# Attention with 16 heads: stacking transfers in three portions around those of the maxima, q and k split sooner, gate rows stored in the first step

## The reference

```python
h = _layernorm(x, axis=-1) * (1 + ca) + sa
q = (x @ Wq + bq).reshape(B, S, H, Dh)
latent = x @ Wl + bl
k = (latent @ Wk + bk).reshape(B, S, H, Dh)
v = (latent @ Wv + bv).reshape(B, S, H, Dh)
scores = jnp.einsum('bihd,bjhd->bhij', q, k) * SCALE
attn = jax.nn.softmax(scores, axis=-1)
out = jnp.einsum('bhij,bjhd->bihd', attn, v).reshape(B, S, D)
out = out @ Wo + bo
x = x + ga * out
```

## Time and profile before

| what | value |
|---|---|
| median of 3 runs | 931.98 us (923.66, 931.98, 932.79) |
| profiled execution | 924.53 us, of which the span of the core 922.8 us |
| PE busy, mean granted clock | 765.3 us (83%), 0.894 |
| DVE / ACT / POOL busy | 633.5 / 538.8 / 390.3 us |
| first attention, steps 2 to 17 | 45.75 to 351 us of the span |

### The profile page before, as it was taken

How to read it: one execution, slowest core, us unless ns; L and a number is a source line. 1 busy time by engine, 2 the same in 40 slices (tenths; PEclk the granted TensorE clock), 3 DMA queues, 4 the chain that set the end, 5 groups by cost and what they waited for, 6 DMA issues and landing times. The chain is left out here.

```text
span 922.8 us, 17153 instructions
## 1 busy us (share of the span) xinstructions
PE 765.3 (83%) x5738; PEld 516.2 (56%) x5738; DVE 633.5 (69%) x1423; ACT 538.8 (58%) x1195; POOL 390.3 (42%) x484
## 2 busy tenths in 40 slices
PE   3378879899778788678999999848999875999996
PEld 3223323233233322277998999836777654887884
DVE  3086775768686664368677776437888875888885
ACT  0215654556465555367788888537888653555553
POOL 3533442443353300014222100058999762776674
PEclk9998886779797886679999999979999996999998
DMA  4255544333443330030000000000000070355430
GB/s 134 36 86 70 69 64 53 47 48 63 57 68 51 49 36 2 15 116 1 2 1 2 1 1 2 1 2 1 2 2 2 1 187 3 104 145 151 115 103 23
DMA packets 81178, 44.19 MB, mean 48 GB/s; under 512 B 7121, under 2 KB 79298, under 8 KB 80962
## 3 DMA queue, kind: packets, MB, share of 16 engines
q1 hardware_dynamic: 81090, 43.07, 24.3%
HBM read 27.83 MB, written 2.25 MB: 33 GB/s over the span
## 5 line engine op out<-in xcount | busy, mean ns | idle before, releaser
L597 DVE TENSOR_REDUCE att_negmax<-att_p_max 128x2 f32<-128x512 f32 x256 | 172.4, 690 | 97.4 <-PE att_p_max L481 93.3
L681 ACT ACTIVATE att_probs<-att_p_sT 128x1024 f32<-128x1024 f32 x128 | 130.9, 1025 | 111.8 <-PE att_p_sT L487 109.4
L481 PE MATMUL att_p_max<-att0p_QK 48*128 48x256 bf16 x512 | 115.6, 325 | 58.6 <-DMA att0p_QK<-att_parts 43.8
L2053 POOL TENSOR_TENSOR moe_z_lo<-moe_z,moe_z_hi 128x512 fp32r<-128x512 f32 x64 | 96.4, 1517 | 56.3 <-ACT moe_z_hi L2006 55.5
L481 PEld LDWEIGHTS att_p_max<-att0p_QK 48*128 48x128 bf16 x512 | 31.0, 100 | 150.3 <-DVE att_negmax L597 61.1
L487 PE MATMUL att_p_sT<-att0p_QK 51*128 51x256 bf16 x512 | 114.5, 324 | 0.0
L509 PE MATMUL att_p_o<-att_probs,att0p_V 128*32 128x256 f32 x1024 | 102.1, 479 | 0.3 <-ACT att_probs L681 0.3
L944 POOL TENSOR_TENSOR ffn0s_rstd<-ffn0s_var_eps,top_minus_half 128x2 f32<-128x2 f32 x16 | 11.2, 700 | 195.3 <-DVE ffn0s_var_eps L931 195.3
L898 PE MATMUL ffn0s_p_h<-ffn0s_u_hi,top_ffn_all 128*128 128x256 f32 x256 | 69.5, 305 | 16.6 <-DVE ffn0s_u_lo L1159 16.2
L1159 DVE TENSOR_TENSOR ffn0s_g_lo<-ffn0s_g,ffn0s_g_hi 128x512 fp32r<-128x512 f32 x64 | 49.1, 782 | 42.5 <-ACT ffn0s_g_hi L1103 41.1
L2044 DVE TENSOR_TENSOR moe_z<-moe_act_u,top_ffn_all 128x512 f32<-128x512 f32 x64 | 74.2, 1160 | 2.2
(11 more groups left out here) (250 smaller groups left out, 2004.8 us busy)
## 6 DMA issues: line engine op xcount, KB each, us to landing
top_ffn_all<-combine SPq DMA_DIRECT2D x32, 512.0 KB, 6.5
att0p_QK<-att_parts SPq DMA_DIRECT2D x192, 64.0 KB
top_X<-in_L_attn_x SPq DMA_DIRECT2D x4, 512.0 KB, 7.1
att_raw<-in_L_ffn_h_w SPq DMA_DIRECT2D x8, 256.0 KB, 4.7
out_x<-top_X SPq DMA_DIRECT2D x8, 256.0 KB, 2.3
top_wo_all<-gates SPq DMA_DIRECT2D x4, 256.0 KB
top_gbo_all<-gates SPq DMA_DIRECT2D x4, 256.0 KB
top_wo_all<-gates SPq DMA_DIRECT2D x1, 1024.0 KB, 6.1
```

The lines of the kernel that those rows point to most:

```text
L481: mm = pe.matmul(bank(at)[:, i, :], QK[r][rows, g, 0, i * P:(i + 1) * P], QK[r][rows, g, 1, :], start=True, stop=True)
L597: dve.tensor_reduce(negmax[:, :, w, g], bank(at)[:], AX.X, ALU.max, negate=True).then_inc(drained, 1)
L681: act.activation(probs[g % 2][:, t % 2], p_sT[t % 2][:], ACT.Exp).then_inc(exped, 1)
L2053: pool.tensor_tensor(z_lo[e % RING][:], z[e % RING][:], z_hi[e % RING][:].bitcast(F32), ALU.subtract).then_inc(z_lo_ready, 1)
```

## The change

`sp_stack` is called in three portions. In step n SP first sends the portions of batch n-1 that need piece 0 and piece 1 (2 and 6 transfers), then the maxima of batch n-3, then the portion that needs piece 2 (4 transfers). The wait for the buffer and for all earlier stacking transfers stands ahead of portion 0. The maxima's two transfers get a semaphore each, the half that PE reads first goes first, and PE waits for each half by itself. ACT makes piece 0 at slot 10, right behind q and k, instead of slot 13. DVE takes the statistics after slot 6 instead of 8. SP stores the gate rows in step 0 instead of step 1.

```diff
-DVE = {"negmax": 0, "out": 5, "stats": 8, "O": 14}
-ACTS = {"OTn": 1, "maxT": 1, "hT": 6, "qk": 10, "OT": 10, "v": 12, "parts": 13}
+DVE = {"negmax": 0, "out": 5, "stats": 6, "O": 14}
+ACTS = {"OTn": 1, "maxT": 1, "hT": 6, "qk": 10, "parts": 10, "OT": 10, "v": 12}
...
-        max_stacked = sem("max_stacked")
+        max_stacked = [sem(f"max_stacked{w}") for w in range(2)]
...
                 if t == 0:
-                    pe.wait_ge(max_stacked, 32 * (sb_ + 1))
+                    pe.wait_ge(max_stacked[sw], 16 * (sb_ + 1))
...
-            at_least(act, max_stacked, 32 * b)
+            for w in range(2):
+                at_least(act, max_stacked[w], 16 * b)
...
+                if slot == ACTS["parts"] and batch_valid(f):
+                    act_parts(act, f, r)
                 if slot == ACTS["OT"] and batch_valid(t):
                     act_OT(act, t)
                 if slot == ACTS["v"] and batch_valid(f):
                     act_v(act, f, r)
-                if slot == ACTS["parts"] and batch_valid(f):
-                    act_parts(act, f, r)
...
-            for w in range(2):
+            for w in (1, 0):
...
-                             ).then_inc(max_stacked, 16)
+                             ).then_inc(max_stacked[w], 16)
...
-        def sp_stack(sp, b, r):
-            at_least(sp, scoredT, PAIRS * (b - NB + 1))
-            at_least(sp, stacked, 16 * STACK_DMAS * b)
-            for part, ready in enumerate((part0_ready, part1_ready, part2_ready)):
-                sp.wait_ge(ready, b + 1)
...
+        def sp_stack(sp, b, r, part):
+            if part == 0:
+                at_least(sp, scoredT, PAIRS * (b - NB + 1))
+                at_least(sp, stacked, 16 * STACK_DMAS * b)
+            sp.wait_ge((part0_ready, part1_ready, part2_ready)[part], b + 1)
...
         def sp_step(sp, n):
+            if n == 0:
+                sp.wait_ge(gate_rows_ready, 1)
+                sp.dma_start(k.gates_dram, gate_rows[:]).then_inc(gates_stored, 16)
+            if batch_valid(n - 1):
+                sp_stack(sp, n - 1, (n - 1) % NB, 0)
+                sp_stack(sp, n - 1, (n - 1) % NB, 1)
             if batch_valid(n - 3):
                 sp_max(sp, n - 3, (n - 3) % NB)
             if batch_valid(n - 1):
-                sp_stack(sp, n - 1, (n - 1) % NB)
+                sp_stack(sp, n - 1, (n - 1) % NB, 2)
             if n == 1:
-                sp.wait_ge(gate_rows_ready, 1)
-                sp.dma_start(k.gates_dram, gate_rows[:]).then_inc(gates_stored, 16)
                 sp.wait_ge(gates_stored, 16)
```

More of the change, by code:

```diff
@@ L733, in term_source @@
                            [[width, HALF], [(3 + k_part - q_part) * S, 2], [1, S]])
-        def sp_stack(sp, b, r):
-            at_least(sp, scoredT, PAIRS * (b - NB + 1))
-            at_least(sp, stacked, 16 * STACK_DMAS * b)
-            for part, ready in enumerate((part0_ready, part1_ready, part2_ready)):
-                sp.wait_ge(ready, b + 1)
[L740 to L746, removed]
-        def sp_step(sp, n):
+        def sp_stack(sp, b, r, part):
[3 more added lines that the diff above has]
+            sp.wait_ge((part0_ready, part1_ready, part2_ready)[part], b + 1)
+            for n, of in enumerate(TERMS):
+                if max(of) != part:
+                    continue
+                for w in range(2):
+                    rows = slice(w * HALF + n * DH0, w * HALF + (n + 1) * DH0)
+                    sp.dma_start(QK[r][rows], term_source(r, w, n)).then_inc(stacked, 16)
+        def sp_step(sp, n):
+            if n == 0:
[4 more added lines that the diff above has]
+                sp_stack(sp, n - 1, (n - 1) % NB, 1)
             if batch_valid(n - 3):
```

## The result

The changed kernel's median is 898.02 us (893.75 to 906.78, four runs) against 932.38 us of the kernel before on the same chip: ratio 0.9655, 95% interval 0.9604 to 0.9705. Some executions of a kernel are 1.5% or more above its fastest; the medians here include them, the ratios leave them out, and where a profiled execution is such a one (sp_order_old and before_poolwait) only the kind of its waits is read from it. The profiled execution of the changed kernel took 898.87 us with a span of 897.1 us, 25.7 us less than the one before.

The account below looks back on a forecast made before the run. A loop through SP (maxima, then twelve stacking transfers) was taken to set the 19.6 us step. 12 x (19.6 - 18.6) plus 1 plus 2 minus 0.5 gave 14.5, say 15 us: 928.2 - 15 = 913 us, range 882 to 933.

Parts of the forecast that it names:

- the stacking wait: PE, first attention: waits for stacking transfers go from every step behind the third, from 43.8 to under 15 us.
- DVE's chain: Step start, four DVE operations meeting POOL's: 2.0 to 2.2 us instead of 1.4, PE waiting 1.8 us at slot 2.
- the clock: PE behind the slot 2 wait: three steps in four lose full clock, at 3.1 us each, adding 2.3 us per step.
- The eight transfers: SP's queue, pieces 0 and 1 ahead of the maxima: cost put at nothing, up to 1 us per step if cover fails.
- my rival "slower": Slot 8: maxima wait behind piece 1's six transfers, slack 0.7 to 2.8 us; 14 us slower, 942 us; chance 7%.
- the step at full clock: Steps 4 to 15: about 16.3 us each if the clock is never lost, with a wait of 1.8 us in it.
- The first steps: Opening steps: 1 us gained together (bounds -2 and +3), with one wait of 1 to 2 us at slot 8.
- Step 16: Late step of about 20 us with a stacking wait of some 2.6 us behind it: 2 us gained.
- the step after it: Step behind step 16: starts with an uncontended chain, no gain, 0.5 us lost.
- the rival that the clock holds: Steps 4 to 15: chain 1.4 us or less, steps 15.7 to 16.3 us, gain 46 us, 882 us; chance 25%.
- The rival that the wait only moves: Steps 4 to 15: every step behaves as step 8, 20.0 us; time 926 to 930 us; chance 13%.

Follow-up runs that it names:

- sp_order_old: Changed kernel with SP's old order, the maxima first and then all twelve stacking transfers: 927.05 us, ratio 0.9943 to the kernel before.
- before_poolwait: Kernel before the change, with POOL waiting at its step's start until ACT has copied the maxima: 931.41 us, ratio 1.0000 to the kernel before.
- the kernel with POOL's wait: Changed kernel, with POOL waiting at its step's start until ACT has copied the maxima: 859.32 us, ratio 0.9212 to the kernel before.

## Why the prediction was right, and where it was short

The mechanism came as forecast: the stacking wait went, DVE's chain took its place, and the clock made it dearer. The range held the time. The gain did not come out as summed: 15 us were forecast, 25.7 lie between the profiled executions and 34.4 between the medians. The largest of the mis-sized terms is the clock's.

*The stacking wait* fell from 43.8 to 8.8 us, all of it ahead of step 4, and SP's old order alone brings the loop back. *The eight transfers stay ahead of the maxima* from step 4 on; costing them at nothing was right only because piece 0 comes sooner, which the version with slot 13 shows with four waits of some 2 us. That was my rival "slower"; it showed in four steps with the transfers 3 us later than they are. Its slack was misworked: six transfers of 1.2 us from 271.7 on have landed by 278.9, not 281.5, so it was 2.8 us and not 0.7.

*DVE's chain* was put at 2.0 to 2.2 us and took 1.99; PE's wait at 1.8 and it is 1.82; the step at full clock at 16.3 and it is 16.2. The rule cited from the Trainium skill (page "SBUF — State Buffer", section "Who interferes with whom") holds here to 0.05 us: L607 ended when L814 did, 1.13 us instead of 0.18. In the kernel with POOL's wait nothing of POOL's runs beside the chain, and L607 takes 0.18 us.

*The clock* was put at three steps in four losing it at 3.1 us each. Eight of the twelve lost it, at (17.3 + 20.1 + 23.2 + 17.7 + 20.0 + 17.6 + 17.7 + 20.1) / 8 - 16.2 = 3.0 us each. So the mean price was right, over single ones of 1.1 to 7.0 us, and the share too high: two in three. Steps 4 and 8, at 15.6 and 15.0 us, are shorter than 16.2 as well: in step 4 the chain met only the end of a POOL operation (0.95 us), in step 8 none. Together that is the 18.06 us measured where I had 18.6. The matmuls that fill the wait show that this term is the clock's. How often a wait of 1.8 us loses the clock I had no row for; three in four was a guess between never and always. That share and mean price both came near is in part luck.

*The first steps* were mis-sized: the wait for the maxima at step 3, put at 1 to 2 us, is 4.9 us. The maxima stand behind eight transfers that left only at 59.4. Still step 4 starts 2.7 us sooner (78.6 against 81.3), 1.4 of it brought along from before step 2. Step 16 gave 0.9 us, not 2; the step after it gained 0.7 instead of losing 0.5.

*The sum.* In the profiled executions 12 x (19.6 - 18.06) = 18.4, plus 2.7, 0.9 and 0.7 makes some 22.8 us, and 2.9 us more lie behind the attention: 25.7 measured against 14.5 forecast. The largest part missing, 6.4 us, lies in steps 4 to 15: 3.5 of it in the term of the clock (12 x 2.3 = 27.6 forecast, 8 x 3.0 = 24.1 measured), 1.8 in the short steps 4 and 8, and the rest in the full-clock step of 16.2 us where I had 16.3. The first steps gave 1.7 us more than forecast, the last two 0.1 more. The 2.9 us are not explained by the change: that part of the program is the same in both kernels, and in its last 140 us the mean granted clock was 0.97 before and 0.99 after. The miss of 15 us in the time itself (913 against 898.02) is these 11.2 us and 3.7 us of the base: I stood the sum on 928.2 us, a mean of four runs, and the profiled execution, from which all rows come, had taken 924.53. The later medians of the kernel before, 932.38, 931.06 and 925.63 us, put most of its runs above that execution, while the changed kernel's profiled execution lies at its median. So the gain between the medians, 34.4 us, is 8.7 us larger than the one that the traces explain, and where these lie no trace here shows. The range held the time, 898.02 in 882 to 933, but it lies just below my own 899 to 922, between the forecast and the rival that the clock holds. The chances were added up too low: 0.55 and 0.25, nearly whole, make nearly 0.80 for faster and not 0.70.

The rival that the wait only moves is refuted as a whole and right in single steps: four of the twelve took 20.0 us or more and gained nothing. The rival that the clock holds was right in the length of four others (15.0 to 16.2 us), but its reason, a chain of 1.4 us or less, held only in two of these; in steps 9 and 13 the chain took 1.99 us and the clock stayed all the same.

## What to carry to other kernels

When a loop of waits is opened, look for what had been running inside its wait at no cost: here a chain of four short DVE operations that met POOL, mostly hidden before and worth 4.6% after. A wait on PE has two prices, its length and the clock behind it, and the second can be the larger: keep waits short, move the other engine's work away from a short chain on the path, and compare steps by their granted clock before explaining their lengths. When a run is to take a cause away, look in its trace whether the cause is gone before reading its time: the wait that cleared POOL from the chain in the changed kernel left it there in the kernel before.

## What the runs showed that was not expected

PE's clock went with the length of the single wait, though not in every case. Waits of 0.6 to 1.1 us at a step's start never lost it; of nine of 1.23 or 1.24 us (piece 0 at slot 13) four were followed by half clock within 2.5 us; those of 1.45 us (kernel before), 1.55 (changed kernel) and 1.59 (kernel before) lost it, at once or within 1.5 us; of nine of 1.82 us seven did and two did not. The half clock lasted some 3, 10 or 17 us for the same wait, so that steps alike in all else took 16.2, 17.6, 20.1 or 23.2 us. What decides between these no run here shows. Idle time can be worth filling: four useless matmuls in each step from 4 on made the kernel 2.4% faster. And the steps became even once the clock held: 15.06 and 16.22 us, eleven and ten times over, to 0.12 us.
